# Layer two of the feed-forward net in one half of the array's rows, v and the output projection in the other; transposes by 64 rows

## The reference

```python
xn = _layernorm(x, axis=-1)
q, k, v = heads of (xn @ w.T * s + b)             # 16 heads of 8
attn = softmax(q k^T / sqrt(8)); ctx = attn v
attention = (ctx @ w_o.T) * s_o + b_o
h = concat([xn, -xn]); h = relu(s0 * h @ (+-1 k0)) * 2      # 256 -> 512
h = relu(s1 * h @ (+-1 k1)) * 2; ffn = s2 * h @ (+-1 k2)    # 512 -> 512 -> 128
x = x + attention + ffn
```

## Time and profile before

| engine | busy us | share of the span | instructions |
|---|---|---|---|
| PE | 273.5 | 93% | 3924 |
| PEld | 185.3 | 63% | 3924 |
| DVE | 246.0 | 84% | 495 |
| ACT | 219.3 | 75% | 456 |
| POOL | 151.0 | 52% | 376 |

### The profile page before, as it was taken

How to read it: one execution, slowest core, us unless ns; L and a number is a source line. 1 busy time by engine, 2 the same in 40 slices (tenths; PEclk the granted TensorE clock), 3 DMA queues, 4 the chain that set the end, 5 groups by cost and what they waited for, 6 DMA issues and landing times.

```text
span 293.0 us, 10539 instructions
## 1 busy us (share of the span) xinstructions
PE 273.5 (93%) x3924; PEld 185.3 (63%) x3924; DVE 246.0 (84%) x495; ACT 219.3 (75%) x456; POOL 151.0 (52%) x376
## 2 busy tenths in 40 slices
PE   4659699999999999999999999999999999999893
PEld 4235375757676776767585867677676758675442
DVE  4654969998989899998989898999999898999522
ACT  2431349889888888979888888888897988777880
POOL 6045446464929293746657382927475575421311
PEclk9557989999999999999999999999999999999999
DMA  5032403232323324142413232332424132320001
GB/s 134 28 122 60 144 19 113 62 111 68 100 76 86 112 58 131 51 126 67 127 36 112 80 106 91 97 101 57 130 60 120 42 106 74 107 74 4 22 22 36
DMA packets 27395, 23.95 MB, mean 82 GB/s; under 512 B 4674, under 2 KB 24146, under 8 KB 27346
## 3 DMA queue, kind: packets, MB, share of 16 engines
q1 hardware_dynamic: 27218, 22.89, 26.2%
q10 hardware_dynamic: 128, 0.39, 0.4%
HBM read 15.47 MB, written 7.34 MB: 78 GB/s over the span
## 4 chain that ended last, share of the span: by engine, by line
PE 88%; DVE 6%; ACT 2%; issue 1%; ACTq 1%; DMA 1%; POOL 0%; POOLq 0%
PE work L984 21%; PE work L1057 20%; PE max_bank L965 14%; PE exp_bank L970 9%; PE work L1089 5%; PE work L1030 4%; PE work L1014 3%; PE work L1098 3%; PE work L1021 3%; DVE neg_max L725 2%; PE work L1010 2%; PE work L999 2%; PE work L992 2%; DVE r_lo L752 1%; PE work L1009 1%
## 5 line engine op out<-in xcount | busy, mean ns | idle before, releaser
L725 DVE TENSOR_REDUCE neg_max<-max_bank 128x2 f32<-128x512 f32 x256 | 167.9, 678 | 22.0 <-PE max_bank L965 18.7
L566 ACT ACTIVATE probs<-exp_bank 128x512 f32<-128x512 f32 x256 | 145.4, 597 | 27.2 <-PE exp_bank L970 22.6
L965 PE MATMUL max_bank<-k_rows,q_rows 48*128 48x256 f16 x512 | 88.7, 271 | 1.5 <-DVE neg_max L725 1.3
L970 PE MATMUL exp_bank<-q_rows,k_rows 51*128 51x256 bf16 x512 | 87.6, 271 | 1.3 <-ACT probs L566 1.2
L984 PE MATMUL work<-probs,v_ext 128*32 128x256 f32 x1024 | 65.0, 383 | 0.2
L1057 PE MATMUL work<-r_hi,w 64*128 64x256 f16 x512 | 61.5, 274 | 0.1
L1057 PE MATMUL work<-r_lo,w 64*128 64x256 f16 x512 | 61.2, 273 | 0.0
L965 PEld LDWEIGHTS max_bank<-k_rows,q_rows 48*128 48x128 bf16 x512 | 40.2, 95 | 25.4 <-DVE neg_max L725 13.8
L970 PEld LDWEIGHTS exp_bank<-q_rows,k_rows 51*128 51x128 f16 x512 | 39.5, 94 | 9.5 <-ACT probs L566 3.3
L752 DVE SCALAR_TENSOR_TENSOR r_lo<-work,r_hi 128x512 f16<-128x512 f32 x64 | 43.3, 679 | 1.7 <-ACT r_hi L619 1.7
L619 ACT ACTIVATE r_hi<-work 128x512 f16<-128x512 f32 x64 | 36.9, 603 | 9.5 <-PE work L1057 3.9
(11 more groups left out here) (105 smaller groups left out, 404.1 us busy)
## 6 DMA issues: line engine op xcount, KB each, us to landing
q_rows<-q_scratch SPq DMA_DIRECT2D x64, 96.0 KB
k_rows<-k_scratch SPq DMA_DIRECT2D x60, 96.0 KB
q_scratch<-q_part SPq DMA_DIRECT2D x16, 192.0 KB, 2.0
xin<-x SPq DMA_DIRECT2D x16, 128.0 KB, 2.2
k_scratch<-k_part SPq DMA_DIRECT2D x16, 128.0 KB, 2.3
out<-outs SPq DMA_DIRECT2D x16, 128.0 KB, 2.6
q_rows<-max_rows SPq DMA_DIRECT2D x64, 6.0 KB
k_rows<-k_scratch ACTq DMA_DIRECT2D x4, 96.0 KB
```

Source lines behind the costliest of these rows:

```text
L566: nc.scalar.activation(probs[h // HALF][:, h % HALF, :, :].rearrange("p k q -> p (k q)"), exp_bank[h % 2][:, :], ACT.Exp, scale=EXP_SCALE) ...
L725: nc.vector.tensor_reduce(out=neg_max[:, h // HALF, h % HALF // 2, h % 2, :], in_=max_bank[h % 2][:, :].rearrange("p (q k) -> p q k", q=TT ...
L965: last = mm(max_bank[h % 2][:, t * SEQ:(t + 1) * SEQ], q[:, t * P:(t + 1) * P], k, start=True, stop=True)
L970: last = mm(exp_bank[h % 2][:, t * SEQ:(t + 1) * SEQ], k[:, t * P:(t + 1) * P], q, start=True, stop=True)
```

## The change

It has five parts.

1. `l2`, `v` and `o` become one job in two phases, `p_0` and `p_1` (`products`). In phase 0 the lower rows compute the lower half of layer two's contraction, 16 float16 products of 64 rows, and the upper rows compute the upper halves of v for the same batch and of the output projection for the batch two earlier. In phase 1 the sides are exchanged. The output projection of the last two batches stays a job of its own.
2. `xT` and `maxT` are done in two phases of 64 rows each, with the matching 64 columns of the result.
3. `xT` has three buffers in place of two, and ACT's copy waits for v of one batch less.
4. The context's reciprocals and its normalisation are issued for each half by itself (`rden0`, `rden1`, `ctxn0`, `ctxn1`).
5. Banks and all order tables are new, and so is the front: q ahead of k, all eight row loads of batch 0 on SP (four were on ACT), and 4 and 22 more dummy transposes (`keep_warm`).

```diff
-PE_AT = {"l1_0": -1, "l0_1": -8, "o": 60, "l0_0": -9, "xT": -20, "ctx0_0": 24, "qk_0": -19, ...
+PE_AT = {"maxT1_0": 19, "p_1": 14, "xT_1": -22, "l0_1": -8, "qk_1": -16, "ctx0_0": 24, ...
...
+            def product_half(name, tokens, w, rows, first):
                 for t in range(TT):
+                    yield mm(psum(name)[:, t * HID:(t + 1) * HID], tokens[rows, t * P:(t + 1) * P], w_sb[rows, w, :],
+                             start=first and t == 0, stop=not first, skip_group_check=True)
+
+            def products(b, phase):
+                if phase == 0:
+                    if b == 0:
+                        pe.wait_ge(w2_ready, 1)
+                    pe.wait_ge(r1_ready, 2 * b + 2)
+                    take_bank("l2", b)
+                    take_bank("v", b)
+                    if b >= 2:
+                        pe.wait_ge(ctxT_ready, b - 1)
+                        take_bank("o", b - 2)
+                else:
+                    pe.wait_ge(products_halved, 2 * (b + 1) if b < 2 else 3 * (b + 1) - 2)
+                rows, other_rows = (LO, HI) if phase == 0 else (HI, LO)
+                layer2 = layer2_half(b, rows, phase == 0)
+                for n, last in enumerate(product_half("v", xT[b % 3], 2, other_rows, phase == 0)):
...
+                    for _ in range(FB):
+                        next(layer2)
+                if b >= 2:
+                    for n, last in enumerate(product_half("o", ctxT, 3, other_rows, phase == 0)):
...
-            def turn_x(b):
-
-                pe.wait_ge(xn_ready, b + 1)
-                bank = take_bank("xT", b)
+            def turn_x(b, phase):
+
+                if phase == 0:
+                    pe.wait_ge(xn_ready, b + 1)
+                    bank, rows, done = take_bank("xT", b), LO, xT_halved
+                else:
+                    pe.wait_ge(xT_halved, b + 1)
+                    bank, rows, done = psum("xT"), HI, xT_psum
                 for t in range(TT):
-                    last = nc.tensor.transpose(bank[:, t * P:(t + 1) * P], xn[:, t, :], ident[:, :])
-                last.then_inc(xT_psum, 1)
+                    first = t * P + phase * TILE
+                    last = nc.tensor.transpose(bank[:, first:first + TILE], xn[rows, t, :], ident[rows, rows])
+                last.then_inc(done, 1)
...
-                at_least(act, v_psum, b - 1)
+                at_least(act, v_psum, b - 2)
...
-            store_k(sp, 0)
-            store_q(sp, 0)
-            load_q(sp, 0)
+            store_q(sp, 0)
+            store_k(sp, 0)
+            load_q(sp, 0)
+            load_k(sp, 0)
...
+            keep_warm(4)
             project_qk(0, 0)
             project_qk(0, 1)
             pe.wait_ge(bv_cols_ready, 1)
             mm(exp_bank[1][:, 0:HID], bv_cols[:, :], w_sb[:, 3, :], start=True, stop=True).then_inc(bias_psum, 1)
+            keep_warm(22)
```

More of the change, by code:

```diff
@@ L43 @@
 EXP_LAG = 17
[L44 to L48, removed]
@@ new lines @@
+ACT_AT = {"xT": -23, "v": 13, "r1a": 5, "max0": 10, "ffn": 14, "r0a": -8, "q": -15, "r1b": 5, "k": -16, "max1": 19, "r0b": -8}
+DVE_AT = {"outs": 46, "r0b": -4, "rden0": 33, "turned0": 26, "rden1": 40, "r0a": -8, "r1a": 6, "r1b": 6, "stats": -32,
+          "turned1": 38, "meanvar": -32, "back": 41}
+POOL_AT = {"ctxn1": 60, "xT_lo": -4, "k_hi": 0, "ctxn0": 52, "norm": -9, "k_lo": 3, "y": 44, "split1": 28, "q_hi": 2,
+           "split0": 25, "q_rest": 3, "q_mid": 3, "q_lo": 5, "xres": -1}
+SP_AT = {"max0": 15, "x": -46, "max1": 23, "rows": -5, "k_store": -15, "out": 60, "q_store": -9}
@@ L1077, in layer1, with layer2_half @@
                     last_b.then_inc(l1_psum, 1)
-            def layer2(b):
-                if b == 0:
-                    pe.wait_ge(w2_ready, 1)
-                bank = take_bank("l2", b)
-                for t in range(TT):
-                    for kk in range(FB):
-                        if kk % 2 == 0:
-                            pe.wait_ge(r1_ready, 2 * b + kk // 2 + 1)
-                        for n, part in enumerate((r1_hi, r1_lo)):
-                            last = mm(bank[:, t * HID:(t + 1) * HID], part[:, kk, t * P:(t + 1) * P], w2[:, kk, :],
-                                      start=kk == n == 0, stop=kk == FB - 1 and n == 1)
-                last.then_inc(l2_psum, 1)
+            def layer2_half(b, rows, first):
+                for t, kk, (n, part) in itertools.product(range(TT), range(FB), enumerate((r1_hi, r1_lo))):
+                    yield mm(psum("l2")[:, t * HID:(t + 1) * HID], part[rows, kk, t * P:(t + 1) * P], w2[rows, kk, :],
+                             start=first and t == kk == n == 0, stop=not first and kk == FB - 1 and n == 1,
+                             skip_group_check=True)
@@ L1128, in _ @@
                         context(b, 1, 1)
-                    elif job == "maxT0":
-                        maxima_to_rows(b, 0)
-                    elif job == "maxT1":
-                        maxima_to_rows(b, 1)
-                    elif job == "xT" and b > 0:
-                        turn_x(b)
+                    elif job == "maxT0_0":
+                        maxima_to_rows(b, 0, 0)
+                    elif job == "maxT0_1":
+                        maxima_to_rows(b, 0, 1)
+                    elif job == "maxT1_0":
+                        maxima_to_rows(b, 1, 0)
+                    elif job == "maxT1_1":
+                        maxima_to_rows(b, 1, 1)
+                    elif job == "xT_0" and b > 0:
+                        turn_x(b, 0)
+                    elif job == "xT_1" and b > 0:
+                        turn_x(b, 1)
                     elif job == "qk_0" and b > 0:
@@ L1138, in _ @@
                         project_qk(b, 1)
-                    elif job == "v":
-                        project_v(b)
-                    elif job == "o":
+                    elif job == "p_0":
+                        products(b, 0)
+                    elif job == "p_1":
+                        products(b, 1)
+                    elif job == "o" and b >= BATCH - 2:
                         project_out(b)
```

169 lines of the change are left out of this document (89 added, 80 removed), and 12 rows, old and new, of tables (DVE_LATER, PE_LATER).

## The result

Four runs of the changed kernel gave 305.67 us in the median (304.45 to 308.4), four of the kernel before 297.35 (295.28 to 298.94): ratio 1.033, 95% interval 1.028 to 1.038. The forecast was 293.5 in a range of 286 to 301. The profiled execution took 306.33 us with a span of 304.5, against 294.85 and 293.0 before. Batches are counted from 0.

A forecast was written before the change was run, and what follows sets the result against it. The rows' way through memory binds: period 0.25 + 6.45 + 8.85 = 15.55 us, above PE's 15.2. Periods −2.2, front and first period −1.2, tail −0.9: −4.3, so 290.55 profiled, 293.5 median; range 286 to 301.

The forecast's parts named there:

- What binds: Projection through q store and row loads to a batch's first scores: sets the period at 15.55 us, above PE's 15.2.
- Projection to q store, 6.45: From a batch's second qk phase to its q store: 6.45 us in place of 7.52, bounds 6.0 to 7.5.
- Store to scores, 8.84: From q store to the batch's first scores: 8.84 us, read from batch 9 and held unchanged.
- The first and last terms I hold: In the period's sum, scores to projection (0.25 us) and store to scores (8.84 us) were taken as unchanged.
- The rival of a chain that is not shortened: Store stays 7.5 us behind the projection, by POOL between q's scaling and last cut: period 16.6, 308.4 us; chance 0.12.
- 16 slots of lead: From a batch's second qk phase to its first scores: 16 slots in place of 18, about 2 us given away.
- PE's 0.69 per batch: PE's saving from pairing and half transposes: 2.75 us removed, 2.06 added; bounds 0.45 to 0.8, PE's period 15.2.
- the second case: The row chain does not bind; PE and DVE set a period of 15.25 us: 289.3 us; chance 0.30.
- DVE: Maxima engine: 14.88 us busy per period plus 0.2 for halved reciprocals gives 15.1, almost as long as PE.
- Front: Start up to first maxima: −0.3 us, range −2 to +0.5; first period another −0.9; −1.2 together.
- End: Tail: halved reciprocals and ctxn start the last context earlier and PE's last batch is shorter: −0.9 us, bounds 0 to −1.5.
- Weight loads in one row group: In layer two's phases on PE, loads do not hide: phase 1.54 us instead of 0.89, 304 to 307 us; chance 0.05.

The follow-up runs named there:

- experiments 1 and 5: Changed kernel with rows loaded from what the batch before stored, loads ahead of stores: 324.27 us; changed kernel with projection and scaling one slot earlier: 304.76 us.
- experiment 8's last version: Changed kernel with result store later, ACT's xT copies one slot later, one k load ahead of the q store, x and a ctxn half later: 307.34 us (1.038).

## Why the prediction was wrong, step by step

In the terms of its sum, the forecast had −4.3 us for the profiled execution and 11.5 came: 15.8 us between them. Of these, 7.5 are waits for rows, 4.2 the end (+3.3 for −0.9), 2.0 PE's own period (−0.2 for −2.2), 1.6 the lower clock behind PE's first wait, and 0.5 the front (−0.7 for −1.2).

- **What binds: right in kind.** The forecast named the way of the rows as the new bound and PE's wait for `q_rows` as its sign. Both are there, and experiments 1 and 5 show the lead to be the cause of these waits: without the row chain no first scores wait, and with one slot of lead more 6.2 us of waits become 0.5.
- **Projection to q store, 6.45: right** (6.57 in the steady batches, with q's last cut at 6.0 and SP still at the maxima's stores; mean 6.55 over batches 2 to 14). Only batches 3 and 5 have 7.60 and 7.26.
- **Store to scores, 8.84: this is the step that failed.** "The first and last terms I hold" took one batch's value, the smallest of the kernel before, for a constant. It is 8.97 to 10.23 now in the batches in which PE waited for the last load, as that load lands 2.74 to 4.50 us after its issue (2.87 to 3.50 before, where all but two batches had slack). A chain without slack pays for each late transfer: 7.5 us, in which batch 5's late store and batch 13's 14 slots have their part. The rival of a chain that is not shortened (308.4) gave nearly the right time, but by another mechanism: its 7.5 us from projection to store occurred in those two batches alone.
- **16 slots of lead: wrong for batch 13,** which has 14. "From the second phase of q and k to the first scores" was read off the steady state and not off the table of shifts.
- **PE's 0.69 per batch: wrong,** and below its own lower bound of 0.45. The products were right (1.80 for 1.78). The 2.75 removed held 0.17 that belongs to the scores around the jobs; the true sum is 2.58. The transposes and the projection cost 0.71 and 1.05 where 0.28 and no change stood, mostly by a wait for ACT. What remains is 0.06. So the second case (289.3) could not have come about even with early rows.
- **DVE: right that it does not bind.** It is busy for 14.83 to 14.93 per steady period, where 15.1 was forecast; the halved reciprocals are 240 ns each instead of one of 333, 0.15 more for the 0.2 taken.
- **Front: −0.7 for −1.2.** The first maxima came at 25.32 instead of 25.97, −0.65 where −0.3 stood, with a granted clock of 0.79 from 8 to 16 us and 0.98 from 16 to 20 (0.53 and 0.50 before). The first period was 0.07 shorter, not 0.9: its clock was 0.67 where it had been 0.89.
- **End: +3.3 for −0.9.** No term stood for the clock there. Two falls of the clock go with the whole of the 3.3, by the ends of the other traces above; the 0.9 did not come either. Why it fell in this kernel and not in the one before is not settled.
- **Weight loads in one row group: refuted,** phases of 0.91 and 0.90. That rival's 304 to 307 holds the measured 305.67, but by luck: its phase of 1.54 did not occur.

## What to carry over

A chain that was hidden by a microsecond must be priced by its latest transfer, not by its typical or its best one, as soon as a change takes its slack; count the slots of lead that a new order gives up, batch by batch and with all shifts, before counting what the engine wins. A job's price on a busy engine is the distance from its own start to the next start, by kind, and not the distance between its neighbours. And two jobs that are joined need all their inputs and banks at once: look who waits for the later of them.

## What was not expected of the hardware

- Two DMAs that each fill 48 partitions, from a source with a repeated outer dimension, landed 9.4 to 10.7 us after issue; four of 24 partitions with the same bytes in all, 2.7 to 4.5. The last completions alone were late, and the packets behind them ran two at a time. Which of the two, the partitions or the repetition, makes it so was not tried.
- After PE's first stand of 1.7 us the granted clock was 0.60 and 0.55 for four us; after later stands of 1.3 and 1.7 us it stayed at 1.00; after two of 2.3 us, in experiment 8's last version, it was 0.50.
- Equal loads of one execution landed 2.74 to 4.50 us after their issue. Moving the result store did not narrow that.
